# Edge attention on a graph: two of each 128 gathered groups loaded row by row from other queues, and a PSUM copy moved from ScalarE to VectorE

## The reference

```python
Q_h = (x @ Wq + bq); K_h = (x @ Wk + bk); V_h = (x @ Wv + bv); E = (edge_attr @ We + be)
score = K_h[src] * Q_h[dst] / sqrt(12) * E
score = exp(clip(score.sum(-1, keepdims=True), -5, 5))     # one number an edge and head
msg = V_h[src] * score
h_out = segment_sum(msg, dst) / (segment_sum(score, dst) + 1e-6)
x = layernorm(x + h_out)
```

## Time and profile before

| | |
|---|---|
| time, median of 3 runs | 4185.39 us (4176.94 to 4186.68) |
| the profiled execution | 4181.88 us, of which the span is 4180.1 us |
| busy | PE 89%, POOL 75%, DVE 53%, ACT 43% of the span |
| granted clock of PE | 0.51 of full speed over the span |
| share of the 16 DMA engines that is busy | about 0.46 in the long stage |
| gathers by POOL | 3224, from 73.7 us to 4106.6 us |

### The profile page before, as it was taken

One profiled execution on the slowest core, in us unless ns is written; L12 is line 12 of the kernel. 1 busy time (PEld: TensorE's weight loads), 2 busy tenths in 40 slices (PEclk: granted clock), 3 DMA queues, 4 the chain that ended last, 5 costly groups with the idle time before them and its releaser, 6 DMA issues.

```text
span 4180.1 us, 67450 instructions
## 1 busy us (share of the span) xinstructions
PE 3715.8 (89%) x20000; PEld 3442.3 (82%) x20001; DVE 2219.6 (53%) x6059; ACT 1795.3 (43%) x4462; POOL 3143.9 (75%) x3361
## 2 busy tenths in 40 slices
PE   8899898888988889889988898888898898889885
PEld 7899888888888888888888888888888888888885
DVE  4755555555555555555555555555555555555556
ACT  3554444444444444444444444444444444444445
POOL 7777777777777777777777777777777777777775
PEclk8555555555555555555555555555555555555555
DMA  8654444444444444444444444444444444444443
GB/s 262 178 143 140 139 130 130 132 137 132 130 131 132 138 130 130 132 136 133 130 130 133 138 130 130 133 137 132 130 131 132 138 131 130 132 136 132 130 122 111
DMA packets 392060, 570.94 MB, mean 137 GB/s; under 512 B 148171, under 2 KB 312444, under 8 KB 392021
## 3 DMA queue, kind: packets, MB, share of 16 engines
q0 software_dynamic: 156832, 321.69, 27.9%
q1 hardware_dynamic: 227763, 237.45, 18.5%
q10 hardware_dynamic: 7426, 11.35, 0.8%
HBM read 547.37 MB, written 22.87 MB: 136 GB/s over the span
## 4 chain that ended last, share of the span: by engine, by line
POOL 61%; issue 21%; DMA 6%; DVE 4%; PE 4%; POOLq 1%; ACT 0%; DVEq 0%; ACTq 0%
POOL kv_mem L620 61%; DMA kv_mem<-kv_table,src_idx 6%; PE bank L735 1%; PE bank L746 1%; DVE kqe L1087 1%; DVE kqe L1084 1%; DVE msg_mem L1100 1%; PE bank L757 1%; DVE y_stats L1193 0%; POOLq L54 0%; DVE oh L1096 0%; POOLq L617 0%; PE bank L740 0%; DVE mean_var L1206 0%; DVE z_inv L1182 0%
## 5 line engine op out<-in xcount | busy, mean ns | idle before, releaser
L620 POOL DMA_INDIRECT kv_mem<-kv_table,src_idx x3224 | 3052.0, 947 | 988.6 <-issue 941.4
L735 PEld LDWEIGHTS bank<-w_e,eaT 97*128 97x128 f32 x6448 | 1440.1, 328 | 626.9 <-issue 587.8
L735 PE MATMUL bank<-w_e,eaT 97*128 97x96 f32 x6448 | 1577.5, 426 | 389.1 <-DVE kqe L1084 384.9
L746 PE MATMUL bank<-oh,msg_mem 128*104 128x32 f32 x6448 | 1255.9, 359 | 3.9 <-DVE msg_mem L1100 3.9
L746 PEld LDWEIGHTS bank<-oh,msg_mem 128*104 128x104 f32 x6448 | 1209.0, 292 | 4.3 <-DVE msg_mem L1100 4.3
L1084 DVE TENSOR_TENSOR kqe<-kv_mem,bank 128x384 f32<-128x384 f32 x806 | 445.8, 553 | 1439.9 <-DMA kv_mem<-kv_table,src_idx 1439.5
L875 ACT ACTIVATE msg_mem<-score 128x32 f32<-128x32 f32 x806 | 184.7, 229 | 2261.9 <-DVE score L1109 2257.9
L757 PE MATMUL bank<-ident,ea_mem 128*96 128x128 f32 x3224 | 858.8, 422 | 10.7 <-DVE bank L1057 7.6
L757 PEld LDWEIGHTS bank<-ident,ea_mem 128*96 128x96 f32 x3224 | 634.2, 225 | 27.9 <-issue 8.2
L885 ACT ACTIVATE away<-off_mem,minus_row 96x512 bf16<-96x512 uint8 x806 | 576.6, 715 | 2.1 <-issue 2.1
L888 ACT ACTIVATE ohT<-away 96x512 bf16<-96x512 bf16 x806 | 507.8, 630 | 25.5
(11 more groups left out here) (98 smaller groups left out, 586.9 us busy)
## 6 DMA issues: line engine op xcount, KB each, us to landing
ea_mem<-in_edge_attr_dram SPq DMA_DIRECT2D x201, 768.0 KB
kv_mem<-kv_table,src_idx POOLq DMA_INDIRECT x3224
off_mem<-offset_by_chunk SPq DMA_DIRECT2D x201, 204.0 KB
q_win<-q_table SPq DMA_DIRECT2D x806, 19.9 KB
kv_table<-kv_mem SPq DMA_DIRECT2D x25, 336.0 KB
q_table<-msg_mem ACTq DMA_DIRECT2D x25, 252.0 KB
x_res<-in_x_dram SPq DMA_DIRECT2D x25, 168.0 KB
out_dram<-kv_mem SPq DMA_DIRECT2D x25, 168.0 KB
```

The source lines that it names most:

```text
L620: pool.indirect_dma_start(kv[:, slot, g, :], None, kv_dram[:, :], bass.IndirectOffsetOnAxis(ap=src_idx[:, u % IDX_RING, g:g + 1], axis=0)) ...
L735: nc.tensor.matmul(e_ps[v][:, g * D:(g + 1) * D], eaT[:, v, g * P:(g + 1) * P], w_e[:, :], start=True, stop=True)
L746: last = nc.tensor.matmul(sums_of(s, v), msg[:, w, g, :], oh[:, w % DEPTH, g, :], start=(g == 0), stop=(g == G - 1), skip_group_check=True)
```

## The change

Of each 32 chunks, chunk 15 and chunk 31 get only three of their four groups from POOL. The 128 rows of the fourth group of chunk 15 are loaded by SP and those of chunk 31 by ACT, one transfer of one row (768 bytes, split in four) each, with the address from a register. SP issues 19 such rows behind each half round (`take_rows`), in calls of at most ten register values (`load_rows`), seven times in 32 steps; the block before has them begin, so that four of these calls for the first chunk 15 stand ahead of the first half round. ACT issues five rows a step in steps 1 to 26 of 32. The source numbers come from `src` in DRAM by one small transfer (`load_row_sources`). Both have one buffer of 128 rows each, and wait for the message of the chunk that used it last. DVE splits lines 1084 and 1100 in two for chunks 15 and 31, and ahead of them waits for all 128 rows.

The copy of the turned attributes (line 881) leaves ACT. DVE makes it instead, behind the message and ahead of the clipping, for the same chunk s+2. The table of base addresses for registers becomes row 0 of the broadcast one, which saves a transfer. The hardware loops of POOL, ACT, DVE and SP have 32 steps instead of 16, POOL's starts at the same step 64; PE's stays as it is.

```diff
+BLOCK = 32
+SP_CHUNK = 15
+ACT_CHUNK = 31
+ACT_GROUPS = 1
+SP_STEP = 19
+ACT_STEP = 5
+ROW_LOAD = 10
...
-        base_tab = sb("base_tab", [1, C], I32)
         base_all = sb("base_all", [P, C], I32)
+        base_tab = base_all[0:1, :]
...
+        gathered = {SP_CHUNK: G - 1, ACT_CHUNK: G - ACT_GROUPS}
+
+        def load_row_sources(engine, chunk, groups, idx, landed_sem):
+            engine.dma_start(idx[:, :].rearrange("a (g p) -> a g p", p=P), src[bass.ds(chunk * CHUNK, CHUNK)].rearrange(
+                "(a p g) -> a g p", a=1, g=G)[:, G - groups:G, :], allow_slow_non_contiguous=True).then_inc(landed_sem, 16)
+
+        def load_rows(engine, first, last, idx, rows, landed):
+            for p0 in range(first, last, ROW_LOAD):
+                count = min(ROW_LOAD, last - p0)
+                nodes = nc.values_load_multi_w_load_instructions(
+                    idx[0:1, p0:p0 + count], engines=(engine.engine,), min_val=0, max_val=N - 1,
...
+                for r, node in zip(range(p0, p0 + count), nodes):
+                    engine.dma_start(rows[r % P:r % P + 1, r // P, :].rearrange("a (r d) -> a r d", r=4),
+                                     kv_dram[bass.ds(node, 1), :].rearrange("a (r d) -> a r d", r=4)).then_inc(landed[r % len(landed)], 16)
...
+            def take_rows(s, u):
+                phase = (u + BLOCK - SP_CHUNK - 1) % BLOCK
+                chunk = s - u + SP_CHUNK + (BLOCK if u > SP_CHUNK else 0)
...
+                if phase == 0:
+                    load_row_sources(sp, chunk, 1, sp_idx, sp_idx_in)
+                else:
+                    k = phase // HALF - 1
+                    if k == 0:
+                        sp.wait_ge(sp_idx_in, ((chunk - SP_CHUNK) // BLOCK if isinstance(s, int) else block_now[0] + 1) * 16 + 16)
...
+                            sp.wait_ge(msg_ready, chunk - BLOCK + 1)
...
+                    load_rows(sp, k * SP_STEP, min(P, (k + 1) * SP_STEP), sp_idx, sp_rows, sp_rows_in)
...
                     load_edges(sp, t, h)
+                take_rows(s, u)
...
             load_edges(sp, 2 * EA_GROUP, 2)
 
+            wait_all(sp, kv_stored)
+            load_row_sources(sp, SP_CHUNK, 1, sp_idx, sp_idx_in)
+            for u in range(SP_CHUNK + 1 + HALF - BLOCK, HALF, HALF):
+                take_rows(u, u)
...
-                for g in range(G):
+                for g in range(gathered.get(u, G)):
...
-            run_steps(pool, step, C, 0, first=4)
+            run_steps(pool, step, C, 0, unroll=BLOCK, first=2)
...
-                k = s + COPY_LEAD
-                if not isinstance(s, int) or 0 <= k < C:
-                    act.wait_ge(ea_flipped, k + 1)
-                    nc.scalar.copy(eaT[0:D, (u + COPY_LEAD) % DEPTH, :], turn_ps[(u + COPY_LEAD) % TURN_DEPTH][0:D, :]).then_inc(ea_turned, 1)
...
+                    lo, hi = (u - 1) * ACT_STEP, min(u * ACT_STEP, ACT_GROUPS * P)
+                    if u >= 1 and lo < hi:
+                        load_rows(act, lo, hi, act_idx, act_rows, act_rows_in)
...
+                    if here < G:
+                        for rows_in in sp_rows_in if u == SP_CHUNK else act_rows_in:
+                            dve.wait_ge(rows_in, block * (8 * P) + 8 * P)
...
+                k = s + COPY_LEAD
+                if not isinstance(s, int) or 0 <= k < C:
+                    dve.wait_ge(ea_flipped, k + 1)
+                    nc.vector.tensor_copy(eaT[0:D, (u + COPY_LEAD) % DEPTH, :], turn_ps[(u + COPY_LEAD) % TURN_DEPTH][0:D, :]).then_inc(ea_turned, 1)
```

More of the change, by code:

```diff
@@ L273, in gnn_kernel @@
         kv_in = [sem(f"kv_in{i}") for i in range(KV_RING)]
+        act_idx_in = sem("act_idx_in")
+        act_rows_allowed = sem("act_rows_allowed")
+        act_rows_in = [sem(f"act_rows_in{i}") for i in range(2 * ACT_GROUPS)]
+        sp_idx_in = sem("sp_idx_in")
+        sp_rows_allowed = sem("sp_rows_allowed")
+        sp_rows_in = [sem(f"sp_rows_in{i}") for i in range(2)]
         pe_step = sem("pe_step")
@@ L482, in _ @@
             load_edges(sp, EA_GROUP, 1)
-            sp.wait_ge(tabs_in, 48)
+            sp.wait_ge(tabs_in, 32)
             sp.wait_ge(pad_stored, 16)
@@ L490, in _ @@
             load_edges(sp, 2 * EA_GROUP, 2)
+            wait_all(sp, kv_stored)
+            load_row_sources(sp, SP_CHUNK, 1, sp_idx, sp_idx_in)
+            for u in range(SP_CHUNK + 1 + HALF - BLOCK, HALF, HALF):
+                take_rows(u, u)
             groups = RING // HALF
-            rounds = (C - AHEAD) // RING
+            rounds = (C - AHEAD) // BLOCK
             lead = AHEAD // HALF
-            for s in range(HALF, RING, HALF):
-                half_round(s, (s // HALF + lead) % groups, None)
+            for s in range(HALF, BLOCK, HALF):
+                half_round(s, (s // HALF + lead) % groups, None, s)
             with sp.Fori(1, rounds) as i:
-                for g in range(groups):
+                block_now[:] = [i]
+                for g in range(BLOCK // HALF):
                     if g % 2 == 0:
[L500 to L503, removed]
+                        bases = load_bases(sp, i * BLOCK + g * HALF + AHEAD)
+                    half_round(i * BLOCK + g * HALF, (g + lead) % groups, bases[g % 2 * HALF:g % 2 * HALF + HALF], g * HALF)
+            for s in range(rounds * BLOCK, C - AHEAD, HALF):
+                half_round(s, (s // HALF + lead) % groups, None, s % BLOCK)
             sp.wait_ge(most_ready, 1)
@@ L868, in _ @@
             act.wait_ge(minus_row_set, 1)
+            wait_all(act, kv_stored)
             def step(s, u, _):
@@ L893, in step @@
                     copy_sources(s + IDX_AHEAD, (u + IDX_AHEAD) % IDX_RING)
-            run_steps(act, step, C, 1, lead=DEPTH, ahead=IDX_RING + EA_GROUP)
+                if not isinstance(s, int) or 0 <= s < WHOLE:
+                    first = s - u
+                    if u == 0:
+                        load_row_sources(act, first + ACT_CHUNK, ACT_GROUPS, act_idx, act_idx_in)
+                    if u == 1:
+                        act.wait_ge(act_idx_in, first // 2 + 16)
+                        act.sem_inc(act_rows_allowed, 1)
+                        if not isinstance(first, int) or first > 0:
+                            act.wait_ge(msg_ready, first)
+                        act.sem_inc(act_rows_allowed, 1)
+                    lo, hi = (u - 1) * ACT_STEP, min(u * ACT_STEP, ACT_GROUPS * P)
+                    if u >= 1 and lo < hi:
+                        load_rows(act, lo, hi, act_idx, act_rows, act_rows_in)
+            run_steps(act, step, C, 1, lead=DEPTH, unroll=BLOCK, ahead=IDX_RING + EA_GROUP)
             def further(c, extra):
@@ L1082, in step @@
                 if scores:
-                    landed(dve, kv_in, a, ua, 16 * G, u)
-                    nc.vector.tensor_tensor(kqe[:, :, :], kv[:, ua, :, 0:D],
-                                            q_ps[u % Q_DEPTH][:, 0:G * D].rearrange("p (g d) -> p g d", g=G), ALU.mult).then_inc(kq_done, 1)
+                    here, block = gathered.get(u, G), a // BLOCK if isinstance(a, int) else block_now[0]
+                    if u in gathered:
+                        before = 0 if u == SP_CHUNK else 16 * gathered[SP_CHUNK]
+                        dve.wait_ge(kv_in[ua], block * (16 * sum(gathered.values())) + (before + 16 * here))
+                    else:
+                        landed(dve, kv_in, a, ua, 16 * G, u)
+                    if here < G:
+                        for rows_in in sp_rows_in if u == SP_CHUNK else act_rows_in:
+                            dve.wait_ge(rows_in, block * (8 * P) + 8 * P)
+                        rows = sp_rows if u == SP_CHUNK else act_rows
+                        nc.vector.tensor_tensor(kqe[:, here:G, :], rows[:, :, 0:D],
+                                                q_ps[u % Q_DEPTH][:, here * D:G * D].rearrange("p (g d) -> p g d", g=G - here), ALU.mult)
+                    nc.vector.tensor_tensor(kqe[:, 0:here, :], kv[:, ua, 0:here, 0:D],
+                                            q_ps[u % Q_DEPTH][:, 0:here * D].rearrange("p (g d) -> p g d", g=here), ALU.mult).then_inc(kq_done, 1)
                     dve.wait_ge(kq_done, a + 1)
@@ L1109, in step @@
                     nc.vector.tensor_scalar(score[:, ua % 2, :], raw_score[:, :], -5.0, 5.0, ALU.max, ALU.min).then_inc(score_ready, 1)
+            block_now = [0]
             def bases_of(i):
                 bases = []
+                block_now[:] = [i]
                 def base_of(u):
                     if u % BASES == 0:
-                        bases[:] = load_bases(dve, i * RING + u - SUM_LAG)
+                        bases[:] = load_bases(dve, i * BLOCK + u - SUM_LAG)
                     return bases[u % BASES]
                 return base_of
-            run_steps(dve, step, C, SUM_LAG, bases_of, lead=1, ahead=DEPTH + EA_GROUP)
+            run_steps(dve, step, C, SUM_LAG, bases_of, lead=COPY_LEAD, unroll=BLOCK, ahead=DEPTH + EA_GROUP)
             def further(c, extra):
```

32 lines of the change are left out of this document (26 added, 6 removed).

## The result

| | |
|---|---|
| time before, median of 4 runs | 4186.03 us (4176.94 to 4189.78) |
| time after, median of 4 runs | 4160.11 us (4151.26 to 4164.89) |
| ratio after to before | 0.9935, 95% interval 0.9923 to 0.9948 |
| the profiled execution after | 4151.26 us, of which the span is 4149.4 us |

The change takes 0.65% off (27 us; from the ends of the interval 22 to 32). Between the two profiled spans it is 30.7 us.

A forecast was written before the change was run, and what follows sets the result against it. POOL's gathers, 1.251 us apart, were taken to bound the kernel. From the profiled 4181.9 us, -62.6 for gathers, +25.7 and +1 at the start, +1 for the copy gave 4147.0; 3.5 to the median gave 4150, range 4138 to 4163.

The forecast's parts named there:

- the 1 us charged for the copy at the end: End of the kernel: DVE's copy of the turned attributes was to cost 1 us in all.
- The gathers, -62.6: POOL's loop: 50 gathers fewer at 1.251 us each, 62.6 us saved.
- The copy, 0.7 us and hidden: DVE, each chunk: the copy moved from ACT takes 0.7 us, at 3.3 of 4.92 us, no cost but some tenths.
- the copy holds POOL up: Rival, all chunks: DVE's copy lengthens POOL's gathers, 320 us more, about 4470; chance 0.05 together with something else.
- A row on SP, 0.435 us: SP's queue: one register-addressed row transfer starts every 0.435 us.
- rows too dear: Rival, SP's start: rows cost too much to issue, no gain at 0.72 us a row; 4172 to 4210, chance 0.13.
- The long stage, no cost: Long stage: SP's rows fit, 15.5 of 19.7 us a half round, and ACT's and DVE's added work costs nothing.
- The start, 25.7 + 1: Start: SP's first rows delay chunk 15, POOL stands 25.7 us at chunk 28, plus 1 us up to step 64.
- One wait of 25 us near 215: Profile sign at the start: POOL has one wait of some 25 us for the message (line 1100) near 215 us.
- ACT's step, 3.95 or 4.7: ACT's step with five rows: 3.95 us, or 4.7 with DVE's register cost; both under 4.92 us a chunk.
- ACT late: Rival, steps 17 to 64: ACT's step is 4.7 us against 4.2 needed, 17 us more, 4167; chance 0.15.
- PE idle from 165 to 240 us: Profile sign at the start: PE is idle between 165 and 240 us.

The follow-up runs named there:

- the last kernel: The change, but POOL gathers the first chunk 15 whole, register loads begin at multiples of four, ACT's first-block rows come four steps later: 4118.39 us, ratio 0.9855.
- The kernel with two half rounds ahead: The change, but SP issues the half rounds of steps 4 and 8 ahead of the rows for the first chunk 15: 4153.27 us, ratio 0.9940.

## Why the prediction came out right, and which term was off

Predicted were 4150 us; measured 4160, the profiled execution 4151.3 against a sum of 4147.0. The time lies inside the stated range of 4138 to 4163, near its upper end. POOL's waits came out 10.6 us larger than the 26.7 that were charged, and the sum missed by only some 4: 3.7 of the waits only take back POOL's earlier start in this execution, and 1.5 from the pitch, 0.2 at the end and the 1 us charged for the copy at the end, which did not come, stand against the rest. That these last 2.7 us offset a part of the miss is luck. The remaining 5.4 us up to the median are that the profiled execution lies 8.9 us below it, where 3.5 was taken.

- **The gathers, -62.6.** 50 fewer at the pitch read before. Shown by the last kernel, which gets 60.8 of 61.3.
- **The copy, 0.7 us and hidden.** 0.680; alone 0.9999. No long gathers beyond those of the first stage, which were there before. The rival "the copy holds POOL up" is refuted by it.
- **A row on SP, 0.435 us.** 0.420, the mean distance of two rows of one register load in SP's records; on ACT 0.435. The rival "rows too dear" needed 0.72. A blocked transfer such as the 2.7 us of the earlier trace rows was never met (0.36 at most on SP, 0.72 on ACT).
- **The long stage, no cost.** Right in what it costs, since POOL's pace is unchanged. But SP's slack was mis-sized: a half round with 19 rows takes 17.1 to 19.0 us and not 15.5, as in most of them the register loads for the rows are 4.4 us (2.27 + 2.14) and not 1.5. It waits 2.7 us a half round on the mean where about 4 was forecast, and catches up mainly in the half round without rows.
- **The start, 25.7 + 1.** This is the term that was mis-sized: 37.3 us. The main mechanism and the place were right: SP's rows for the first chunk 15 stand ahead of the loads. Undoing it gives 32 us back. Of the 10.6 us, 4.6 is a later restart: chunk 28's first gather begins at 246.44 us, and by the prediction it would have been 216.1 + 25.7 = 241.8. A further 3.7 is the earlier start of POOL in this execution (its wait ends with the same event however early it comes to it), 1.25 the gather of chunk 15 that is gone ahead of chunk 28, which I had left out, and 0.7 the wait at chunk 64 above the 1 us allowed. The rest, 0.3, is open.
- **Where the 4.6 us come from.** Two things. SP's rows are 2.55 us later: DVE starts on them at 240.55 instead of 238. Up to the end of the first four calls SP is 3.4 us behind (188.25 against 184.9), roughly the sum of a start 5.4 sooner (the first register load begins at 140.3, not 145.7), rows 0.8 cheaper (0.425 us each in these calls), and register loads 9.7 dearer: 46.59 - 76 x 0.425 = 14.3 us for seven of them and 1.4 ahead of the first row, 15.7 where I had 6.0. The rest is 1.8 more in the three half rounds and 2.6 less for landing. And the event was another one: POOL doesn't wait for the message of chunk 14 (over at 243.0, 2.4 after the forecast) but for ACT's copy of source numbers behind the exponentials of chunk 15, which puts POOL 3.4 us behind that message instead of 1.2.
- **One wait of 25 us near 215.** This step failed: three waits, at 155, 194 and 246 us. I had followed only DVE and POOL behind SP's late half round and not ACT, which needs its offsets first and carries POOL's source numbers in the same queue. What I had written of ACT's queue, that only the exponentials and `ohT` stand behind the rows, left this copy out. The kernel with two half rounds ahead shows that this moved the waiting and didn't add to it, since the same total has to be waited for in any case. The 4.35 at 155 us comes from ACT's own rows: its steps take 4.5 us there (143.58 to 148.11 in its timeline); the last kernel, without rows in these steps, takes 3.2 and waits 0.6. POOL's earlier start is a part of it too: the kernel with the copy alone has no rows at all, and waits 1.1 there.
- **ACT's step, 3.95 or 4.7.** 4.0 when the load begins at a multiple of four values, 4.5 otherwise, 4.6 with the copy of sources. I took SP's kind of register load; mostly it was DVE's kind. The rival "ACT late" put 17 us on it; the kernel after pays 1.7, probably since PE's own pace there (205.94 of 210 us busy) is not much faster; that was not tried by itself. With half a microsecond more, the copy left on ACT, POOL pays 14.9 there, close to the rival's 17. The threshold lay between.
- **PE idle from 165 to 240 us.** In part: it is busy 36.92 of these 75 us. It stands 26.7 us for attributes up to 198.8, works, and stands 13.2 us up to 243.7.

## What to carry to other kernels

Work taken off the bounding engine pays only where the queues that now carry it start it in time: here a periodic job cost nothing in 24 blocks of 25, and its first instance, put whole ahead of the first chunks' loads, cost 32 us of 62.6, which one gather more (1.25 us) bought back. When a queue is delayed, follow each of its consumers, and add up nothing that one late producer causes twice: only the time of its last item counts. Measure an engine's step against the stretch with the thinnest cover: moving the copy was worth nothing alone and some 15 to 18 us once ACT issued rows.

## What the runs showed of the hardware

**A register load costs by where it begins.** Medians of line 462 in the kernel after, by the first value's place in the table of source numbers (worked out from its records):

| queue, values | begins at | median |
|---|---|---|
| SP, 4 | 124 | 0.57 us |
| SP, 9 | 48 | 1.03 us |
| SP, 10 | 0 or 76 | 1.15 us |
| SP, 9 | 10 | 2.14 us |
| SP, 10 | 19 | 2.27 us |
| ACT, 5 | multiples of 4 | 0.72 us |
| ACT, 5 | others | 1.30 us |

All places are of 4 bytes, so the cheap ones begin at a multiple of 16 bytes. Beginning at a multiple of 8 bytes is no cheaper than elsewhere (places 38 and 114: 2.26 us). It also fits that the same load of eight values took 0.70 us on SP and 1.85 on DVE before: DVE's begins five chunks back (`SUM_LAG`), so not at such a multiple; no run here loads DVE's registers from another place. On SP and ACT the kernel with aligned loads confirms it: 0.72 and 0.74, 13 us of waits fewer. The Trainium skill, "Runtime: NRT & Kernel Launch", section "Instruction fetch mechanics", puts a register at some 200 ns even when many are loaded. It says so of loads from HBM, and the tables here are in SBUF. The rows come near that figure for loads that begin elsewhere (2.27 us for ten) and are at about half of it for aligned ones (1.15).

**The longer loops fetch their code again.** Code packets (queue q14) rose from 23 to 448 with loops of 32 steps on POOL, ACT, DVE and SP and the rows written out in them; without SP's rows they are 306, and the copy alone, in loops of 16, keeps 23. Once a turn DVE and ACT pause some 4 to 5 us with no releaser. Two rows of the timeline of the kernel after:

```profile
2006.82 0.23 ACT L939 ACTIVATE msg_mem<-score 128x32 f32<-128x32 f32 x1 [4.57 <-issue]
...
2008.79 0.19 DVE L1155 TENSOR_TENSOR accT<-bank,accT 104x32 f32 x1 [4.41 <-issue]
```

The same section of the Trainium skill says that a taken branch whose target lies outside the engine's window of code has to fetch it first; the count of packets agrees, and so does the place of the pause: ACT's records have the loop's branch (line 69) at 2001.68 us and nothing more until 2006.73. Here POOL has no wait in the long stage, so it costs nothing; that it is what makes these pauses was not tried by itself.
